# A four-layer gated transformer on one core: the last layer's softmax denominators by way of DRAM, its tokens in bf16 parts, its steps in another order

## The reference

```python
def _mosa_branch(X, router_w, wqkv, wo):          # 8 heads, 64 wide
    k = t // 8                                     # 64 tokens of 512 for each head
    scores = jnp.einsum('bth,hn->bnt', X, router_w)
    _, idx = jax.lax.top_k(scores, k); idx = jnp.sort(idx, axis=-1)
    gates = sigmoid(take(scores, idx))
    Xg = X at idx
    Q, K, V = split(einsum('bnkh,hnd->bnkd', Xg, wqkv), 3)
    Q, K = _rope(Q, pos=idx), _rope(K, pos=idx)   # the first 32 of 64 columns are turned
    AV = softmax(causal(Q K^T / 8)) V * gates
    out = zeros.at[bi, hi, idx].set(AV)           # back to their places
    return out @ wo
def _dense_branch(X, wqkv, wo):                   # 8 heads, all 512 tokens, causal
    Q, K = _rope(Q, arange(t)), _rope(K, arange(t))
    return (softmax(causal(Q K^T / 8)) V) @ wo
```

## Time and profile before

| | |
|---|---|
| median of 3 runs | 493.73 us (493.62 to 495.23) |
| the profiled execution: its time, its span | 496.68 us, 494.9 us |
| PE matmul busy | 450.1 us, 91% of the span |
| DVE, ACT, Pool busy | 279.7, 220.6, 111.7 us |
| the last layer's feed-forward part | from 342.5 us to the end |
| DMA | 16.17 MB, 281 GB/s at the start, about 23 GB/s in the last layer |

### The profile page before, as it was taken

The page is one execution under the profiler, slowest core; times in us unless marked ns, Lnnn a source line. Parts: engine busy times, 40 slices in busy tenths (PEclk is TensorE's granted clock), DMA queues, the critical chain, the costliest instruction groups (busy, mean ns, idle before and its releaser), DMA issues.

```text
span 494.9 us, 7761 instructions
## 1 busy us (share of the span) xinstructions
PE 450.1 (91%) x3062; PEld 276.1 (56%) x3067; DVE 279.7 (57%) x588; ACT 220.6 (45%) x442; POOL 111.7 (23%) x98
## 2 busy tenths in 40 slices
PE   5999999989999899987999999989889989899986
PEld 3634443566765544776655775864345544666452
DVE  2665684486555565786235663544467753465561
ACT  3145656334102354454243325532378755467360
POOL 1300000230101103543000006000255551493300
PEclk9999999999998999999999999999999999899999
DMA  8800000270000000000000002000011111111000
GB/s 281 362 2 1 2 1 0 64 265 2 0 1 0 1 0 2 1 1 1 1 0 0 1 2 85 1 1 0 1 21 23 22 23 19 27 23 23 1 21 23
DMA packets 5493, 16.17 MB, mean 33 GB/s; under 512 B 1489, under 2 KB 2386, under 8 KB 4946
## 3 DMA queue, kind: packets, MB, share of 16 engines
q1 hardware_dynamic: 5458, 15.68, 10.3%
HBM read 13.06 MB, written 0.52 MB: 27 GB/s over the span
## 4 chain that ended last, share of the span: by engine, by line
PE 67%; DVE 18%; issue 6%; ACT 4%; POOL 3%; DMA 1%; SPq 0%; DVEq 0%; ACTq 0%; POOLq 0%
PE PS L537 57%; PE PS L1175 2%; PE PS L802 2%; DVE mxd L2200 2%; DVE mx L1762 2%; DVE wmoe L1755 2%; POOL rstd L2403 2%; PE PS L569 2%; ACT wmoe L1596 1%; DVE keys L1880 1%; PE PS L630 1%; DMA cols<-cols_dram 1%; ACT PT L1429 1%; DVE PS L2193 1%; POOL wmoe L2433 1%
## 5 line engine op out<-in xcount | busy, mean ns | idle before, releaser
L2403 POOL TENSOR_TENSOR rstd<-veps,mhalf 128x4 f32<-128x4 f32 x16 | 16.4, 1035 | 242.2 <-DVE veps L1700 242.2
L537 PE MATMUL PS<-PTB,keys 128*64 128x128 f32 (+3 forms) x384 | 41.2, 377 | 0.0
L1596 ACT ACTIVATE wmoe<-PS,mxd 128x512 f32<-128x512 f32 (+3 forms) x64 | 33.2, 534 | 4.7 <-DVE mxd L2200 4.5
L1880 DVE TENSOR_REDUCE keys<-PS 128x9 f32<-128x693 f32 x32 | 26.5, 872 | 8.6 <-PE PS L537 8.6
L1608 ACT COPY PTB<-PS 128x768 f32<-128x768 f32 (+1 forms) x24 | 20.9, 873 | 23.2 <-PE PS L1175 23.0
L537 PE MATMUL PS<-cst 128*128 128x512 f32 (+2 forms) x66 | 30.0, 566 | 0.4 <-DVE x L1720 0.4
L1374 ACT ACTIVATE sq<-PS 128x512 f32<-128x512 f32 x16 | 9.6, 598 | 44.3 <-PE PS L537 44.3
L537 PE MATMUL PS<-va,PT 128*128 128x72 f32 (+2 forms) x224 | 28.4, 277 | 1.0 <-ACT PT L1429 1.0
L537 PEld LDWEIGHTS PS<-PTB,keys 128*64 128x64 f32 (+2 forms) x384 | 20.8, 145 | 14.5 <-issue 11.6
L537 PEld LDWEIGHTS PS<-va,PT 128*128 128x128 f32 (+1 forms) x224 | 26.4, 191 | 3.0 <-ACT PT L1429 2.0
L537 PE MATMUL PS<-keys,PTB 32*128 32x231 f32 (+2 forms) x448 | 27.1, 327 | 0.3 <-DVE wmoe L1776 0.3
(11 more groups left out here) (349 smaller groups left out, 937.8 us busy)
## 6 DMA issues: line engine op xcount, KB each, us to landing
wmoe<-w_dram SPq DMA_DIRECT2D x2, 2048.0 KB, 11.8
den<-wmoe SPq DMA_DIRECT2D x28, 64.0 KB, 2.3
wa<-wa_dram SPq DMA_DIRECT2D x4, 256.0 KB, 13.4
wlate<-ew_dram SPq DMA_DIRECT2D x2, 512.0 KB, 5.3
wd<-wd_dram SPq DMA_DIRECT2D x1, 1024.0 KB, 9.2
wlate<-wm_dram SPq DMA_DIRECT2D x1, 1024.0 KB, 4.8
cst<-const_dram SPq DMA_DIRECT2D x1, 754.5 KB, 7.7
cst<-const_dram SPq DMA_DIRECT2D x1, 551.0 KB, 5.4
```

What stands on the lines that cost most here:

```text
L537: return nc.tensor.matmul(o, l, r, start=start, stop=stop, skip_group_check=True)
L1596: A_(PR[n % 2][:, z, to:to + (t + 1) * 128], PS[:, ring_banks("turn", n).start + z, to:to + (t + 1) * 128], ACT.Exp, bias=mxd[:, n % 2, k, ...
L1880: last = v.tensor_reduce(mxn[:, 2 * half + t, :].rearrange("p (g r) -> p g r", r=32)[:, :, 12:15], PS[:, at:at + NG, t * 256:t * 256 + GK] ...
L2403: g.tensor_tensor(rstd[:, b, :], veps[:, b, :], mhalf[:], ALU.pow).then_inc(S("ln_rstd"), 1)
```

## The change

1. The opening of the layer. ACT, Pool and DVE work in another order for pair 0: Pool multiplies the keys by their cosines ahead of `root(7, 1)`; DVE adds the swapped products to queries and keys together, in one instruction, behind its own products. PE runs scores(0) ahead of values(0), and the keep_clock between them is gone. ACT copies values(3) ahead of exps(0). DVE's rounds of top move: round 0 behind the maximum of step 1, rounds 1 to 3 into iteration 1.
2. Tokens in bf16 parts. For each batch Pool splits `htok` into three bf16 parts (high, middle, low; `split`), and gather multiplies all three by the upper halves of the one-hots' f32 words, 12 bf16 products instead of 4 in f32. split(0) stands ahead of rope(1), split(1) behind rope(2). Both batches' one_hots are made in iteration 7.
3. `turns` is divided into `cosines` and `sines`, 64 rows wide for each batch, with one copy each for all 128 partitions; the copy of the cosines adds 1 to the rows that aren't turned. The memsets of `trig` are gone.
4. Denominators of pairs 0 to 6: SP sends the reciprocals to DRAM, element by element, so that they lie there by head and token, then reads each head's 512 values back over 64 partitions (`share`); Pool multiplies (`norm`, behind rope(r + 3), the last ones behind rope(7)). The last pair's still go through widened, spread and DVE. share(r - 2) stands in SP's queue behind the swap of pair r, and ahead of the sparse swap where r = 5; share(6) stands ahead of the stores of the output.
5. `FILL` is written anew; y of batch 0 is divided into y0 and y, and `dense` moves to the end of iteration 19.

```diff
-        4: (("values", 7), None, ("spread", 0)),
-        6: (None, (0, "columns"), None),
+        6: (("values", 7), (0, "columns"), None),
         7: ((0, "ranks"), None, None),
-        9: (None, ("spread", 1), (0, "gather")),
-        10: ((0, "angles"), (1, "gather"), (1, "angles")),
-        11: ((0, "turns"), None, (0, "q")),
-        12: ((0, "k"), ("spread", 2), (0, "slots")),
-        13: ((0, "v"), None, ("spread", 3)),
-        15: ((0, "scores"), None, None),
-        16: ((0, "weights"), None, ("spread", 4)),
+        8: (None, None, (0, "gather")),
+        9: ((0, "angles"), None, (1, "gather")),
+        10: ((1, "angles"), None, (0, "cosines")),
+        11: ((0, "sines"), None, (0, "q")),
+        12: ((0, "k"), None, (0, "slots")),
+        13: ((0, "v"), None, None),
+        15: (None, None, (0, "scores")),
+        16: (None, (0, "weights"), None),
         17: ((0, "sums"), None, None),
         18: ((0, "out0"), None, (0, "out1")),
-        19: (None, (0, "dense"), None),
-        20: ((0, "y"), None, ("spread", 5)),
-        22: (None, None, ("spread", 6)),
+        19: (None, None, (0, "dense")),
+        20: ((0, "y0"), None, None),
+        21: ((0, "y"), None, None),
         23: (None, None, ("spread", 7))}
...
+            def share(r):
+
+                sp.wait_ge(S("d_recip"), r + 1)
+                sp.dma_start(shares[r].rearrange("(c p) -> p c", p=128), recs[:].rearrange("p z t -> p (z t)"), allow_slow_non_contiguous=True).then_inc(S("d_sent"), 16)
+                sp.wait_ge(S("d_sent"), 16 * (r + 1))
+                if r > 0:
+                    sp.wait_ge(S("d_normed"), r)
+                for z in range(2):
+                    sp.dma_start(shared[64 * z:64 * z + 64, :], shares[r, z * T:(z + 1) * T].partition_broadcast(64)).then_inc(S("d_shared"), 16)
...
                 for at in (0, 16, 64, 80):
                     sp.dma_start(SW[r % 2][at:at + 16], QK[r % 2][at ^ 16:(at ^ 16) + 16]).then_inc(S(f"d_moved_{r % 2}"), 16)
+                if r >= 2:
+                    share(r - 2)
                 if r == 5:
...
+            share(PAIRS - 2)
...
                     elif s == "gather":
                         pe.wait_ge(S(f"sp_G{b}"), TB - b)
-                        for t in range(TB):
-                            last = mm(PS[:, 7, :], htok[:, b * TB + t, :], OH[b][:, t, :], start=(t == 0), stop=(t == TB - 1))
+                        pe.wait_ge(S("sp_parts"), 4 * (b + 1))
+                        for n, part in enumerate(tparts[b]):
+                            for t in range(TB):
+                                last = mm(PS[:, 7, :], part[:, t * 128:(t + 1) * 128], OH[b].bitcast(BF16)[:, t, 1:1024:2],
+                                          start=(n == 0 and t == 0), stop=(n == 2 and t == TB - 1))
...
                 pe.wait_ge(S("sp_work"), 1)
                 values(1, 7)
+                pe.wait_ge(S("d_swap"), 4)
+                scores(0)
                 pe.wait_ge(S("sp_htok"), 1)
                 values(0, 6)
-                keep_clock(3, 512, 512)
-                pe.wait_ge(S("d_swap"), 4)
-                scores(0)
                 ln_spread(7, 1)
...
+                values(3, 3, 7)
                 exps(0)
-                values(3, 3, 7)
                 pair(1)
...
-                    if n % 3 == 1 and n > 3 and n // 3 - 1 < LATE:
-                        widen(n // 3 - 1)
...
+                    dve.wait_ge(S("d_raw"), 1)
+                    v.tensor_tensor(first, first, C3("ropec"), ALU.mult).then_inc(S("d_first"), 1)
...
-                    v.tensor_tensor(first, first, SW[0][:, 0, :], ALU.add).then_inc(S("d_first"), 1)
+                    dve.wait_ge(S("d_roped"), 1)
+                    v.tensor_tensor(both, both, SW[0][:], ALU.add).then_inc(S("d_first"), 1)
...
-                    elif s == "turns":
+                    elif s == "cosines":
                         product()
-                        for c in range(B):
-                            for j in range(2):
-                                ins = v.tensor_copy(trig[64 * c:64 * c + ROT, j, :], PS[64 * c + ROT * j:64 * c + ROT * j + ROT, 7, :])
-                        ins.then_inc(S("sp_taken"), 1)
+                        v.tensor_scalar(trig[:, 0, :], PS[:, 7, :], C3("plain"), None, ALU.add).then_inc(S("sp_taken"), 1)
+                    elif s == "sines":
+                        product()
+                        v.tensor_copy(trig[:, 1, :], PS[:, 7, :]).then_inc(S("sp_taken"), 1)
...
-                    for k in ((1, 2), (3,), (4,), (5,), (6,), (7,))[n] if n < 6 else ():
+                    for k in ((0,), (1, 2, 3), (4,), (5,), (6,), (7,))[n] if n < 6 else ():
                         top(k)
...
+                split(0)
+                def norm(r):
+
+                    b, q = divmod(r, 4)
+                    pool.wait_ge(S("d_shared"), 32 * (r + 1))
+                    pool.wait_ge(S("d_taken"), r + 1)
+                    g.tensor_tensor(AVT[:, b, q, :], AVT[:, b, q, :], shared, ALU.mult).then_inc(S("d_normed"), 1)
+
                 for r in range(1, PAIRS):
                     rope(r)
+                    if r >= 3:
+                        norm(r - 3)
+                    if r == 2:
+                        split(1)
                     if r == 5:
                         sparse_rope()
+                for r in (PAIRS - 3, PAIRS - 2):
+                    norm(r)
```

More of the change, by code:

```diff
@@ L75 @@
 PLACED = 98
-LATE = 5
 CODE = 512
@@ L167, in copied @@
     return name, before(a, name) + len(mine) * u + mine.index(j) + 1
-POOL_SET = dict(mhalf=1, first=8, iota=10, ones=18, mbias=19, mask3=20, last=26)
+POOL_SET = dict(mhalf=1, first=8, iota=10, ones=18, mbias=19, mask3=20, last=22)
 def before(a, name):
@@ L269, in constants @@
                 turns[32 * n + k, half * z + k] = 1.0
-                turns[32 * n + half + k, ROT + half * z + k] = (-1.0, 1.0)[z]
-    turns[96:98, 64] = 1.0
+                turns[32 * n + half + k, HP + half * z + k] = (-1.0, 1.0)[z]
+    turns[96:98, 2 * HP] = 1.0
+    put3("plain", p[:, None] % HP >= ROT)
     put3("turns", paired(turns))
@@ L432, in build @@
         tab = C3("tab").bitcast(BF16)
+        early = wqk0[:].rearrange("p z r -> p (z r)")
+        tparts = [[early[:, 256 * b:256 * b + 256].bitcast(BF16), (sw2[:].rearrange("p j d -> p (j d)"), mbias[:].rearrange("p t k -> p (t k)")[:, 0:256])[b].bitcast(BF16),
+                   (early[:, 512:768], wf1[:].rearrange("p n d -> p (n d)")[:, 0:256])[b].bitcast(BF16)] for b in range(B)]
         turns = C3("turns", 0, PLACED).bitcast(BF16)
@@ L1228, in sparse @@
                                       OH[b].bitcast(BF16)[:, t, 1:1024:2], start=(t == 0), stop=(t == TB - 1))
-                    elif s == "turns":
+                    elif s in ("cosines", "sines"):
+                        at = 0 if s == "cosines" else HP
                         for c in range(B):
-                            last = mm(PS[half[c], 7, :], turns[:, 0:64], placed[c])
+                            last = mm(PS[half[c], 7, :], turns[:, at:at + HP], placed[c])
                     elif s in ("q", "k"):
@@ L1270, in sparse, with heads_out @@
                             mm(PS[:, 7, :], wod[:, q, :], AVT[:, 0, q, :], start=(q == 0), stop=False)
-                    elif s == "y":
-                        last = heads_out(0, 7, False, True)
-                    if s != "dense":
+                    elif s in ("y0", "y"):
+                        last = heads_out(0, 7, False, s == "y", *((0, 2) if s == "y0" else (2, 4)))
+                    if s not in ("dense", "y0"):
                         last.then_inc(S("last_y" if s == "y" else "sp_product"), 1)
-                def heads_out(b, bank, start, stop):
+                def heads_out(b, bank, start, stop, first=0, end=4):
                     pe.wait_ge(S("sp_taken"), made(0, "out1"))
                     pe.wait_ge(S("sp_masks"), 4 * (b + 1))
-                    for q in range(4):
+                    for q in range(first, end):
                         last = mm(PS[:, bank, :], spz[b][:, q, :], GT[b][q], start=(start and q == 0), stop=(stop and q == 3))
@@ L2204, in rope_queries @@
                 def rope_queries():
-                    first = QK[0][:, 0, :]
+                    both = QK[0]
+                    first = both[:, 0, :]
+                    dve.wait_ge(S("d_raw"), 1)
+                    v.tensor_tensor(first, first, C3("ropec"), ALU.mult).then_inc(S("d_first"), 1)
                     dve.wait_ge(S("pool_set"), POOL_SET["last"])
-                    dve.wait_ge(S("d_swapped"), 1)
+                    dve.wait_ge(S("d_pair"), 3)
                     for j in range(4):
@@ L2322, in filler @@
                 def filler(f):
-                    if f in (None, (0, "dense"), ("spread", PAIRS - 1)) or f[0] == "values":
+                    if f in (None, (0, "dense"), (0, "y0"), ("spread", PAIRS - 1)) or f[0] == "values":
                         return
```

(13 more changed lines are left out.)

105 lines of the change are left out of this document (47 added, 58 removed).

## The result

The changed kernel takes 495.83 us (median of 17 runs, 492.6 to 498.57) where the kernel before, measured beside it, takes 493.3 (17 runs, 491.69 to 496.64). The ratio is 1.0049, with a 95% interval of 1.0026 to 1.0072: slower by half a per cent, where I forecast 485.2 us and gave "slower" a chance of 0.13. The profiled execution also took 495.83, with a span of 494.0. The one of before took 496.68, so it lay 3.4 us above the median of its kernel. That shows in where the layer begins: at 342.50 before and at 339.26 after, by the same six products. So the comparison that follows counts from the layer's own start. By it the last product ends 149.2 us in before (491.66) and 151.5 us in after (490.74): 2.3 us slower, as the medians say.

A forecast was written before the change was run, and what follows sets the result against it. TensorE's list of work, two thirds of the span, was taken as the bound. Terms 4.3 + 1.2 + 3.0 + 3.3 - 3.5 + 0.2 = 8.5 us off 493.73 gave 485.2 us, range 480 to 491.5.

The forecast's parts named there:

- The transfer of a share: Seven sends of 1024 single 4-byte elements to DRAM, each taken to land in 3.5 us, between bounds 2.0 and 12.9.
- the end of the cover: Send time up to which other work hides the transfer, so that nothing waits: 6.8 us.
- three places: Swap(3), the sparse swap and norm(6), said to have no cover left once a send takes 6.8 us or more.
- its rival's formula: Slow-send rival, chance 0.13: three places each lose L - 6.8 us for send time L; gain gone at 9.6.
- Swap(3): Swaps standing behind the waiting SP queue, said to be late only if a send takes 6.8 us or more.
- the opening: Layer start up to scores(3): reordered work on Pool, DVE and PE gains 4.3 us, or 3.1 if exps stay the limit.
- the gathers: Steps 8 to 10: each gather as 12 bf16 products takes 2.8 us for 3.6, saving 0.8 each.
- the wait for the sine table: Steps 11 and 12 up to k: PE's 2.7 us wait and the slow-clock stretch behind it go; stage gains 3.3 us.
- The casts: Pool's copies for splitting tokens, taken at 0.8 us each, with 1.26 for each subtraction; 4.1 us a batch.
- Steps 2 to 7: Spread(0) leaves PE and values(7) moves to step 6: PE's busy 23.7 us become 23.1, gain 1.2.
- the new hole at the sparse scores: Steps 12 to 16: Pool's sparse sum comes late behind SP's order, PE stands still 3.6 us; stage loses 3.5.
- 480 as a rival: The sparse swap isn't late: 3.5 us not lost, 1.2 gained, clock stays up, 480 us; chance 0.12.

The follow-up runs named there:

- e2: The changed kernel with the reciprocals sent as 128 rows of 32 bytes, denominators read back in the wrong order: 486.21 us, ratio 0.9867.
- e8: The changed kernel with reciprocals sent as rows of 32 bytes and the sparse swap issued ahead of share(3): 479.55 us, ratio 0.9718.
- e1: A kernel of small transfers alone, each awaited before the next: the changed kernel's send takes 11.7 us, the same 4 KB as rows 1.4.
- e10: A kernel of small transfers alone, 1024 elements written 4, 8, 16, 32 and 64 B apart: 11.7, 4.7, 3.4, 3.1 and 2.6 us.
- e9: The changed kernel with each sent element 64 B from its neighbour, reads taken from x instead: 484.89 us, ratio 0.9859.
- e7: The changed kernel, slow send kept, with two tiles of reciprocals used in turn: 501.16 us, ratio 1.015.
- e3: The changed kernel, slow send kept, with a share's reads behind the next pair's swaps on SP and the send behind these reads: 493.83 us, ratio 1.0016.

## Why the prediction was wrong

Gains over before in us, counted from the layer's start (scores begin at 28.3, 52.9, 73.9 and 107.9 us in before; the last product ends at 149.2). The forecast column sums its terms.

| up to | forecast | changed | e2, fast send | e8, fast send, swap first |
|---|---|---|---|---|
| scores(3) | 4.3 | 4.1 | 4.1 | 4.1 |
| scores(9) | about 5.5 | 1.8 | 4.7 | 4.7 |
| scores(12) | 8.5 | 3.6 | 8.0 | 8.0 |
| k's copy on Pool | 11.8 | 7.0 | 11.4 | 11.3 |
| scores(18) | 8.3 | 2.7 | 6.5 | 12.0 |
| last product | 8.5 | -2.3 | 7.4 | 12.9 |

**The step that failed** is the one under "The transfer of a share": "I take 3.5, near the store, as the queue is now empty". The send takes 8.3 to 10.8 us. The bounds, 2.0 and 12.9, held it; the choice between them didn't. I weighed the number of pieces and the state of the queue. What decides is a third thing, that single elements (here from 128 partitions) land side by side in DRAM (11.7 us on an idle chip in e1, and 2.6 at 64 B apart in e10). The 3.5 would have been fair for elements that lie apart: e9's take 2.8.

**What hung on it was in order.** The prediction put the end of the cover at 6.8 us and named three places. With 10.3 in its rival's formula the time is 493.73 - 8.5 + 3 x 3.5 = 495.7, and 495.83 was measured. That the total agrees so well is partly luck, since the places differ:
- Swap(3): right. Scores(9) wait 2.8, and the clock behind them costs 1.5 more (19.10 us to scores(12), 17.64 in e8).
- The end: right place, other wait. I looked at norm(6) alone and took the last reciprocal as free. It writes the tile that the seventh send still reads, and waits 6.9 us; that single tile isn't in my steps at all. The wait that I did name is real: in e7, with a send of 11.5 us, the formula's steps (0.6 + 11.5 + 1.2 + 1.9 + 1.3, less the cover of 11.8) give a wait of 4.7 for norm(6), and 4.9 was measured. The last window is 30.98 us, e8's is 25.10: 5.9 lost.
- ACT's wait for "remote" in step 14: overlooked. Scores(12) to (15) take 18.47 us, in e8 15.46: 3.0 lost. ACT stands so in the changed kernel (3.6), in e7 (4.1) and, a copy earlier and under another name, in e3 (6.6), the three with slow sends, and in no kernel with a fast send or none. What holds it up stays open.
- The sparse swap: it is late, but by then PE is late too, so only 1.4 of the 4.7 of e2 is seen, and 3.6 us of the loss so far come back by scores(18).

Loss against e2: 2.9 + 1.5 + 3.0 - 3.6 + 5.8 = 9.6 us, which is what the medians give.

**Right, by the runs:** the opening (4.3 forecast, 4.1 measured, with 1.23 us for the sum of both halves instead of 1.4), the gathers (2.8 us), the wait for the sine table gone and with it the stretch at 1.2 GHz (up to k's copy 11.8 forecast, 11.4 in e2). The casts took 0.61 for my 0.8 and the subtractions 1.16 for 1.26; splitting delayed nothing that PE waited for in e2. Steps 2 to 7 gave 0.6 instead of 1.2: from scores(3) to scores(9) PE is busy for 23.5 us of 24.1 in e8, where I had 23.1 with less of a hole.

**Right in kind, too small:** the new hole at the sparse scores. From k's copy Pool needs 431.44 - 412.48 = 19.0 us in e2, for 18.8 forecast. (My 1.9 for the last swap's landing behind its issue should have been 2.3 - 0.6 = 1.7 by the rows that I named; it changes nothing here.) PE gets there 14.5 us after it (431.59 - 4.66 - 412.48), for 15.2: so 4.7 us for 3.6. The hole with the clock behind it costs 6.7 us (e8 against e2) where I had 3.5 lost, 1.2 not gained and 0.7 for the clock, 5.4. Without it I had 480 as a rival; e8 is 479.55.

The Trainium skill, DMA: Bandwidth & Descriptors, puts a plain DMA with a rearranged access pattern at 19 times the hardware's DMA transpose, under Rules for kernel authors. No run here has that transpose; against rows the rearranged send was 8 times as slow (11.7 to 1.4 us in e1), so the direction of that warning was right, and I gave it too little weight. The about 10.5 ns a packet that the Trainium skill gives on the same page, under Bandwidth, for loads, and which I turned into an estimate of 2.7 us, agrees with 1024 elements 64 B apart (2.6) and misses those side by side by a factor of four.

## What to carry to other kernels

A transfer that no trace shows, between bounds of 2 and 13 us, with the end of its cover in between, is worth more chance for the slow case than 0.13. Before trusting a store of small pieces, ask where each piece lands: give rows, or turn the data over first (a small DVE instruction and three more issues a pair bought 9.4 us here). A slow transfer can be felt in more places than its own reader: the queue behind it, the tile that it reads from, and, as ACT in step 14, an engine that neither reads nor writes its data; list the writers of the source tile as well as the readers of the destination. And when one queue carries transfers of two chains, the order of issue is a term of its own (6.7 us for one moved block).

## What the runs showed of the hardware

- 1024 elements of 4 bytes from 128 partitions to DRAM take 9.3 to 11.7 us side by side, 4.7 at 8 B apart, 3.4 at 16, 3.1 at 32, 2.6 to 3.6 at 64; into SBUF 2.3; as 128 rows of 32 B 1.4. 256 of them from 128 partitions take 8.5, 128 from 16 partitions 1.4.
- While such a store was on its way, four swaps issued by SP took 5.4 us instead of 2.4 (e3), and ACT stood with its operands ready: 3.6 and 4.1 us for "remote" (the changed kernel, e7), 6.6 for "issue" (e3). That this is ACT's code being loaded late is a reading that no run here isolates; the one instruction load that shows beside the wait (16 KB, from 422.1 in the changed kernel) kept its DMA engine busy for 1.3 us, as the like one in e2, where ACT doesn't wait.
- Behind the long waits of PE named here stands a stretch partly or wholly at 1.2 GHz. Behind scores(9) the mean granted clock is 0.64 for 4.0 us (transposes 1.54 us for 0.87), behind scores(15) 0.65 for 4.9 us, behind the last spread 0.68 for 5.3 us (products 5.3 for 3.6), behind norm(6) in e7 0.50 for 5.5 us, and behind the wait at e2's sparse scores 0.57 for 4.9 us. That last wait, 4.7 us long, cost 6.7 in all.
